# Latents and values of an attention layer in column and row tiles of TensorE

## The reference

```python
q = x @ W_q; k = x @ W_k; v = x @ W_v            # D = 256
latent_kv = (k + v) @ W_down_kv                  # 64 numbers a token
k_rec = (latent_kv @ W_up_k)                     # 16 heads of 16
v_rec = (latent_kv @ W_up_v)
scores = einsum("bhqd,bhkd->bhqk", qh, k_rec) / sqrt(d) * decay
attn = softmax(scores)
out = einsum("bhqk,bhkd->bhqd", attn, v_rec) @ W_o
```

## Time and profile before

| what | value |
|---|---|
| median of the runs | 5883.54 us |
| the profiled execution | 5887.21 us |
| its span, first to last instruction | 5885.3 us |
| mean granted TensorE clock | 0.971 of full speed |
| instructions | 114753 |
| ScalarE busy | 56% of the span |
| VectorE busy | 78% of the span |

### The profile page before, as it was taken

The page is one execution under the profiler, slowest core; times in us unless marked ns, Lnnn a source line. Parts: engine busy times, 40 slices in busy tenths (PEclk is TensorE's granted clock), DMA queues, the critical chain, the costliest instruction groups (busy, mean ns, idle before and its releaser), DMA issues.

```text
span 5885.3 us, 114753 instructions
## 1 busy us (share of the span) xinstructions
PE 5403.7 (92%) x35920; PEld 3230.8 (55%) x35920; DVE 4596.3 (78%) x14385; ACT 3307.3 (56%) x6581; POOL 2830.4 (48%) x2873
## 2 busy tenths in 40 slices
PE   5559999389999999999999999999999999699997
PEld 5558888133444444444444444444444444588886
DVE  7735555577888888888888888888888887555776
ACT  1124444146666666666667666666676666344443
POOL 6740000253647657566475564765756433300455
PEclk9999999688999999999999999999999999799998
DMA  5533333543545555555455454555554543433777
GB/s 173 171 109 105 105 105 102 137 99 77 135 99 129 115 113 123 108 120 126 100 125 115 111 132 103 127 115 111 129 106 111 111 81 67 149 104 119 233 245 228
DMA packets 538508, 731.84 MB, mean 124 GB/s; under 512 B 80281, under 2 KB 454209, under 8 KB 537921
## 3 DMA queue, kind: packets, MB, share of 16 engines
q1 hardware_dynamic: 488768, 590.22, 41.5%
q0 software_dynamic: 49152, 134.28, 7.7%
HBM read 426.70 MB, written 297.53 MB: 123 GB/s over the span
## 4 chain that ended last, share of the span: by engine, by line
PE 70%; POOL 15%; DVE 6%; issue 4%; DMA 3%; SPq 1%; ACT 1%; POOLq 0%; DVEq 0%; ACTq 0%
PE psum L396 13%; PE psum L1315 13%; PE psum L1166 13%; PE psum L1175 10%; PE psum L413 7%; POOL xs L658 4%; PE psum L1179 3%; DVE at_mx L1456 3%; PE psum L385 2%; PE psum L404 2%; POOL at_xT L1616 2%; PE psum L1223 2%; POOL at_Sd L1694 2%; DMA at_xT<-ys,at_yib 2%; POOL at_XR L1625 1%
## 5 line engine op out<-in xcount | busy, mean ns | idle before, releaser
L1379 ACT ACTIVATE at_P<-psum 128x512 f32<-128x512 f32 x4096 | 2125.7, 602 | 981.5 <-PE psum L1175 565.5
L1456 DVE TENSOR_REDUCE at_mx<-psum 128x4 f32<-128x512 f32 x3584 | 2219.1, 681 | 266.1 <-PE psum L1166 260.4
L1166 PE MATMUL psum<-at_kst,at_qst 96*128 96x128 bf16 (+3 forms) x7168 | 1599.0, 293 | 52.3 <-DVE at_mx L1456 29.4
L1175 PE MATMUL psum<-at_qst,at_kst 99*128 99x512 bf16 (+3 forms) x5120 | 1463.5, 319 | 53.8 <-ACT at_P L1379 53.7
L1166 PEld LDWEIGHTS psum<-at_kst,at_qst 96*128 96x128 bf16 x7168 | 617.9, 99 | 1319.4 <-DVE at_mx L1456 509.4
L1315 PE MATMUL psum<-at_P,at_V 128*17 128x512 f32 x8192 | 1092.5, 605 | 0.0
L1694 POOL TENSOR_TENSOR at_Sd<-at_Sd,at_m 128x1024 f32<-128x1024 f32 x256 | 484.2, 1897 | 819.1 <-DVE at_m L1465 818.1
L1175 PEld LDWEIGHTS psum<-at_qst,at_kst 99*128 99x128 bf16 x5120 | 491.4, 98 | 198.8 <-ACT at_P L1379 85.5
L1179 PE MATMUL psum<-at_ident,at_Sd 128*128 128x128 f32 x2048 | 565.8, 276 | 0.0
L1451 DVE CUSTOM_DVE_ANT_0 at_Sd<-psum,at_Dm 128x128 f32<-128x128 f32 x2048 | 443.1, 287 | 90.3 <-PE psum L1166 90.1
L699 POOL DMA_INDIRECT m2Y<-ys,m2yi x256 | 246.8, 964 | 511.5 <-ACT m2X L456 434.0
(11 more groups left out here) (267 smaller groups left out, 8125.5 us busy)
## 6 DMA issues: line engine op xcount, KB each, us to landing
parts<-at_pt SPq DMA_DIRECT2D x768, 128.0 KB
at_qst<-parts SPq DMA_DIRECT2D x768, 128.0 KB
at_kst<-parts SPq DMA_DIRECT2D x128, 384.0 KB
m2X<-xs SPq DMA_DIRECT2D x288, 128.0 KB, 2.4
ys<-m2X SPq DMA_DIRECT2D x288, 128.0 KB, 1.7
m1X<-xs SPq DMA_DIRECT2D x264, 128.0 KB, 2.1
ys<-m1X SPq DMA_DIRECT2D x264, 128.0 KB, 1.7
at_kst<-parts SPq DMA_DIRECT2D x128, 256.0 KB
```

The source lines that it names most:

```text
L1166: ins = e.matmul(bank[z % 4][:, col - 512 * u:col - 512 * u + ln], self.qst[0:96, s, side, 128 * t:128 * t + 128], self.kst[0:96, s, 1 - s ...
L1175: ins = e.matmul(turns[a % 3][:, q0 - 512 * qh:q0 - 512 * qh + ln], self.kst[0:99, s, side, 128 * kb:128 * kb + 128], self.qst[0:99, s, 1 ...
L1379: e.activation(self.P[:, i % NP, 512 * qh:512 * qh + 512], turns[a % 3], ACT.Exp).then_inc(self.taken.sem, 1)
L1456: e.tensor_reduce(self.mx[:, p % 2, hh, 8 * o + 4 * u:8 * o + 4 * u + 4], of, op=ALU.max, axis=AX.X).then_inc(self.s_read.sem, 1)
```

## The change

One latent unit for each batch instead of two. Its eight matmul instructions write the two halves of the partitions of one bank: half ch of the tokens goes to partitions 64 ch to 64 ch + 63 (two column tiles), and lat becomes 128 partitions x 512. The weights W_up_k and W_up_v are loaded twice, into both halves of the partitions. Keys read lat and the weight from the half that belongs to ch, still one bank at a time. Values are issued in pairs: tile t2 of the first half and tile 2 + t2 of the second, as two row tiles that write two turning banks; TensorE waits for one more bank to be read (taken.at(a - 1)), and ScalarE's copies wait until both are filled. The plan has one slot less for latents, and the values stay in four slots, with work in the first and third of them.

```diff
--- before.py
+++ after.py
@@ -719,7 +719,7 @@
         self.qst, self.kst = sb("qst", [99, 2 * NS, 2, S], BF16), sb("kst", [99, 2 * NS, 2, S], BF16)
         self.P, self.Sd = sb("P", [128, NP, S]), sb("Sd", [128, 4, 8, 128])
         self.V = sb("V", [128, 2, 8, H, 17])
-        self.XR, self.xT, self.lat = sb("XR", [128, 8, D]), sb("xT", [128, 2, S]), sb("lat", [DL, S])
+        self.XR, self.xT, self.lat = sb("XR", [128, 8, D]), sb("xT", [128, 2, S]), sb("lat", [128, 512])
         self.qs = sb("qs", [128, 2, 2, 512])
         self.pt = sb("pt", [128, 2, 3, 2, 512], BF16)
         self.OT, self.OF = sb("OT", [128, 2, 8, D]), sb("OF", [128, 2, 512])
@@ -729,7 +729,7 @@
         self.ident, self.Dm = sb("ident", [128, 128]), sb("Dm", [128, 128])
         self.decay = sb("decay", [128, 2, S])
         self.wq, self.wk, self.wo = sb("wq", [128, 2, D]), sb("wk", [128, 2, D]), sb("wo", [128, 2, D])
-        self.wd, self.wuk, self.wuv = sb("wd", [128, 2, DL]), sb("wuk", [DL, D]), sb("wuv", [DL, D])
+        self.wd, self.wuk, self.wuv = sb("wd", [128, 2, DL]), sb("wuk", [128, D]), sb("wuv", [128, D])
         self.wv = self.Ou[:, 0].rearrange("p (k d) -> p k d", k=2)
         self.wT = self.ob[:, 0]
         self.wkv = sb("wkv", [128, 2, DL])
@@ -757,7 +757,7 @@
         self.number()
 
 
-        self.loaded, self.x_in = sig.new("a_loaded", 16 * 15), sig.new("a_x_in", 48 * B)
+        self.loaded, self.x_in = sig.new("a_loaded", 16 * 17), sig.new("a_x_in", 48 * B)
         self.y_in, self.x1_out = sig.new("a_y_in", 256 * B - 128), sig.new("a_x1_out", 16 * B)
         self.y_first = sig.new("a_y_first", 128)
         self.m_out, self.parts_out = sig.new("a_m_out", 16 * NPAIR), sig.ring("a_parts_out", [96 * 4 * B] * 2)
@@ -898,8 +898,7 @@
             yield ("load", b + 1)
 
     def unit_order(self, b):
-        for ch in range(2):
-            yield from (("latent", b, ch), None)
+        yield from (("latent", b), None)
         if not b:
             for i in range(0, 8, 2):
                 yield from (("project", 0, i), ("project", 0, i + 1))
@@ -907,18 +906,18 @@
                     yield from (("cast", 0, i, c), ("cast", 0, i + 1, c), ("rest", 0, i, c), ("rest", 0, i + 1, c))
                 yield from (("send", 0, i), ("send", 0, i + 1))
                 if i == 2:
-                    yield from (("values", 0, t2) for t2 in range(4))
+                    yield from (("values", 0, t2) for t2 in (0, 2, 1, 3))
             return
         for i in range(8):
             yield from (("project", b, i), None, ("cast", b, i, 0), None, ("rest", b, i, 0))
             if i:
                 yield ("send", b, i - 1)
             yield from (None, None, ("cast", b, i, 1), None, ("rest", b, i, 1), None)
-        for t2 in range(4):
-            yield ("values", b, t2)
-            if t2 == 2:
+        for t2 in range(2):
+            yield from (("values", b, t2), ("values", b, 2 + t2))
+            if t2 == 1:
                 yield ("send", b, 7)
-            yield None
+            yield from (None, None)
 
     def norm_order(self, p):
         yield from (None, ("norm", p))
@@ -1069,8 +1068,8 @@
         self.load_tokens(e, 0)
         for dst, src in ((self.ident[:], cst["ident"]), (self.decay[:, 0], cst["decn"]), (self.decay[:, 1], cst["decp"]),
                          (self.Dm[:], cst["dm"]), (self.wq[:], fold(wt["q"])), (self.wk[:], fold(wt["k"])),
-                         (self.wv, fold(wt["v"])), (self.wd[:], fold(wt["down"])), (self.wuk[:], wt["upk"]),
-                         (self.wuv[:], wt["upv"]), (self.wo[:], fold(wt["o"])),
+                         (self.wv, fold(wt["v"])), (self.wd[:], fold(wt["down"])), (self.wuk[0:DL], wt["upk"]), (self.wuk[DL:128], wt["upk"]),
+                         (self.wuv[0:DL], wt["upv"]), (self.wuv[DL:128], wt["upv"]), (self.wo[:], fold(wt["o"])),
                          (self.trif[:], cst["tri"]), (self.misc[:], cst["misc"]), (self.rw[:], fold(wt["rw"])),
                          (self.rb[:], wt["rb"].rearrange("(o n) -> o n", o=1).to_broadcast([128, E]))):
             e.dma_start(dst, src).then_inc(self.loaded.sem, 16)
@@ -1154,7 +1153,7 @@
         NS, NP, V = self.NS, self.NP, bank[4]
         turns = bank[5:8]
         fence(w, self.begin)
-        w.wait_ge(*self.loaded.at(240))
+        w.wait_ge(*self.loaded.at(272))
         w.wait_ge(*self.w_ready.at(2))
 
         def scores(n, o, u, z):
@@ -1204,11 +1203,12 @@
                     ins = e.transpose(to[:, 128 * t:128 * t + 128], self.XR[:, 4 * ch + t, 128 * k:128 * k + 128], self.ident[:])
                 ins.then_inc(self.filled.sem, 1)
             if kind == "latent":
-                b, ch = at
+                b = at[0]
                 w.wait_ge(*self.result("weight", 2))
-                w.wait_ge(*self.result("turn", b, ch, 1))
+                w.wait_ge(*self.result("turn", b, 1, 1))
                 for k in range(2):
-                    ins = e.matmul(to[0:DL, 0:512], self.wkv[:, k, :], self.xT[:, k, 512 * ch:512 * ch + 512], start=(k == 0), stop=(k == 1))
+                    for ch in range(2):
+                        ins = e.matmul(to[DL * ch:DL * ch + DL, :], self.wkv[:, k, :], self.xT[:, k, 512 * ch:512 * ch + 512], start=(k == 0), stop=(k == 1))
                 ins.then_inc(self.filled.sem, 1)
             if kind == "project":
                 b, i = at
@@ -1222,16 +1222,21 @@
                     for k in range(2):
                         ins = e.matmul(of, self.wq[:, k, 128 * hf:128 * hf + 128], self.xT[:, k, sl], start=(k == 0), stop=(k == 1))
                 else:
-                    w.wait_ge(*self.result("latent", b, ch))
-                    ins = e.matmul(of, self.wuk[:, 128 * hf:128 * hf + 128], self.lat[:, sl], start=True, stop=True)
+                    w.wait_ge(*self.result("latent", b))
+                    ins = e.matmul(of, self.wuk[DL * ch:DL * ch + DL, 128 * hf:128 * hf + 128], self.lat[DL * ch:DL * ch + DL, :], start=True, stop=True)
                 ins.then_inc(self.s_filled.sem, 1)
             if kind == "values":
                 b, t2 = at
-                w.wait_ge(*self.result("latent", b, t2 // 2))
-                for j in range(2):
-                    t = 2 * t2 + j
-                    ins = e.matmul(to[:, 256 * j:256 * j + 256], self.lat[:, 128 * t:128 * t + 128], self.wuv[:], start=True, stop=True)
-                ins.then_inc(self.filled.sem, 1)
+                if t2 < 2:
+                    w.wait_ge(*self.result("latent", b))
+                    w.wait_ge(*self.taken.at(a - 1))
+                    for j in range(2):
+                        t = 2 * t2 + j
+                        for half, to in ((0, turns[a % 3]), (1, turns[(a + 1) % 3])):
+                            ins = e.matmul(to[:, 256 * j:256 * j + 256], self.lat[DL * half:DL * half + DL, 128 * t:128 * t + 128],
+                                           self.wuv[DL * half:DL * half + DL, :], start=True, stop=True)
+                            if j == 1:
+                                ins.then_inc(self.filled.sem, 1)
             if kind == "mturn":
                 p = at[0]
                 w.wait_ge(*self.m_max.at(p + 1))
@@ -1337,13 +1342,13 @@
                 w.wait_ge(*self.added.at(2 * b + 2))
                 if b:
                     w.wait_ge(*self.turned_read(b - 1))
-                    w.wait_ge(*self.full("latent", b - 1, 1))
+                    w.wait_ge(*self.full("latent", b - 1))
                 e.activation(self.xT[:, k, 512 * ch:512 * ch + 512], of, ACT.Copy).then_inc(self.taken.sem, 1)
             if kind == "latent":
-                b, ch = at
+                b = at[0]
                 if b:
                     w.wait_ge(*self.full("values", b - 1, 3))
-                e.activation(self.lat[:, 512 * ch:512 * ch + 512], of[0:DL, 0:512], ACT.Copy).then_inc(self.taken.sem, 1)
+                e.activation(self.lat[:], of, ACT.Copy).then_inc(self.taken.sem, 1)
             if kind == "cast":
                 b, i, c = at
                 j = 8 * b + i
@@ -1352,6 +1357,7 @@
                 e.activation(self.pt[:, j % 2, c], self.qs[:, i % 2], ACT.Copy).then_inc(self.part_hi.sem, 1)
             if kind == "values":
                 b, t2 = at
+                w.wait_ge(*self.full("values", b, 2 + t2 % 2))
                 if b >= 2:
                     w.wait_ge(*self.weighed.at(64 * (b - 1)))
                 e.activation(self.V[:, b % 2, 2 * t2:2 * t2 + 2, :, 0:16], of[:, 0:512].rearrange("p (t h d) -> p t h d", t=2, h=H), ACT.Copy).then_inc(self.taken.sem, 1)
```

## The result

The changed kernel takes 5844.2 us (median of 6 runs, 5838.3 to 5855.9), the kernel before, run beside it, 5882.3 us (6 runs, 5878.4 to 5884.4). The ratio is 0.9937, with a 95% interval of 0.9926 to 0.9948: 38 us faster. Forecast were 65, and 5818 us; the measured time lies in the range of 5785 to 5860. The direction held, and so did the latents and most of the pairs; the term for what moves did not.

What follows compares the result with a forecast made beforehand. TensorE was taken to pace most of a batch and GpSimd one stretch; latents 27.9 + 1.8, values 20.4 and what moves 15.4 sum to 65.5 us saved, from 5883.54 to 5818 us, range 5785 to 5860.

Steps and rivals of the forecast that it cites:

- What bounds the kernel: Attention batches: TensorE paces most steps, GpSimd one stretch of some 55 us; TensorE time saved shortens the batch one for one.
- Latents: Merged latent unit on TensorE takes 1.86 us, as one old unit; saves 27.9 us in batches 1 to 15, 1.8 in batch 0.
- (b): Rival: weight loads stand between the column tiles' passes, 16.8 us less saved, 5835 us; chance 0.06.
- (e): Rival: tiles don't run beside each other at all, no saving in latents either, 5876 us; chance 0.04.
- Values: Each pair on TensorE saves 1.05 us less a new wait of 0.37 us: 0.68 us, 20.4 us for 30 pairs.
- rival (a): Row tiles of the values don't overlap; pairs cost +0.32 us instead of -0.68, 5848 us; chance 0.13.
- Rival (c): GpSimd's stretch gets the whole benefit and pairs wait less: -45.5 us instead of -15.4, 5788 us; chance 0.12.
- What moves: One latent slot fewer moves later units a step earlier, changing GpSimd's stretch by -1.1 us a batch, -15.4 us in 14.
- The weakest step named: ScalarE's wait before the cast of project 5 grows, and that is paid back later in GpSimd's stretch.
- Rival (d): The rest of project 6 on GpSimd ends no earlier, as gathers, sends and stack collide: 5903 us; chance 0.07.

Runs made afterwards that it cites:

- g2: The kernel before with both latent units in one slot, so only the plan's shift changes: 5899.4 us, ratio 1.0032, where the kernel before takes 5880.9 us.
- g1: The changed kernel with r_var's addition on GpSimd and the pairs of values behind W: 5825.9 us, ratio 0.9905 to the kernel before.
- h1: The changed kernel with an empty slot behind the latents, r_var's addition on GpSimd and values behind W: 5839.8 us, ratio 0.9919 to the kernel before.
- 6100 groups: Groups of runs in which the kernel before takes some 6100 us (6091.6 and 6111.7 us).
- f3: The changed kernel with r_var's addition moved from VectorE to GpSimd: 5966.3 us, ratio 0.9764 to the kernel before.
- 5880 group: A group of runs in which the kernel before takes some 5880 us.
- the second group: Runs of the changed kernel, in-place part, shift alone and r_var on GpSimd: 5996.0, 6065.2, 6040.4 and 5966.3 us; the kernel before takes 6111.7 us.
- the fourth group: Runs of the changed kernel with empty slot, r_var on GpSimd and values behind W, and with latent loops exchanged: 5839.8 and 5863.7 us; before, 5886.5 us.

## Why the prediction was half right

**What bounds the kernel: right.** TensorE time saved in its regime came off one for one. In the two steps that held latents each batch is 1.9 us shorter.

**Latents: right,** 1.87 us for eight matmuls against 1.86 taken. Rivals (b) and (e) fall with these rows. The Trainium skill's rule on weight loads, which spoke against the change ("TensorE: Matmul & The Clock Gate", Part 3), isn't borne out: with its eight loads between the passes the unit would have been 2.98 us.

**Values: right in kind.** Row tiles overlap as W's column tiles do (1.07 us for eight matmuls), so rival (a) falls. The wait was 0.44 us instead of 0.37: a pair saves 1.05 - 0.02 - 0.44 = 0.59 us, and 30 pairs 17.7, not 20.4. Rival (c) falls too: it wanted shorter waits for the pairs and 3.25 us off a batch for what moves.

**What moves: this step failed.** The forecast was -15.4 us, with bounds of +1.05 and -3.25 a batch; measured alone it is **+18.5 us** (interval +11 to +26), and a batch in steady state is 2.0 us longer, outside the bounds. The step followed the rest of project 6 through GpSimd's queue and the gathered rows through DMA, and both did what it said: that rest ends some 7 us earlier in its batch (5 without the projection that moved across the batch's start), and the add's wait (us, times) fell from

```profile
  DMA at_xT<-ys,at_yib: 35.1, 18
```

in the kernel before to

```profile
  DMA at_xT<-ys,at_yib: 11.8, 2
```

in the changed one. But the sum took the stretch to be as long as that rest decides, and it isn't. TensorE's waits for ScalarE, which hang on the rests, were 31.9 us in 13 batches and fell by 11; its waits for VectorE were 37.4 us and grew by 28. Of VectorE the step said that its small stalls "shift with it: I leave them at zero, bounds +-0.4 us a batch". That sentence was the error, and the trace of before spoke against it: beside the 0.35 us that it read, there was a wait of up to 2.4 us for the maxima in each batch (L1263 above). The add pair moved into a step in which r_stats runs, and there VectorE's r_var waits until GpSimd's add is through, some 2 us, with the maxima and TensorE behind it. The waits come with the shift alone (g2). With r_var on GpSimd the 2.4 us of step 16 are gone (g1), and the shift costs nothing (h1 against g1); both are shown, though both kernels also have the pairs behind W. r_var alone was moved only in 6100 groups, where it gives 30 us (f3). That these waits are all of the shift's cost is not shown: when r_var left, m waited longer in f3, and the stretch of steps 20 to 31 grew in g1 and h1, by 2.1 and 1.5 us.

The Trainium skill has this behaviour ("SBUF — State Buffer", section "Who interferes with whom"): a VectorE instruction with two SBUF inputs, or one such as tensor_scalar in a mode that uses two ports, contends with GpSimd, and the one that is issued later is blocked for the other's whole instruction. The trace agrees for r_var, which ends 0.02 us after the add; in which mode it ran no row shows. A reader of that section would have looked for GpSimd's longest instructions beside each such VectorE instruction. The forecast didn't.

**The weakest step named** was another: that ScalarE's wait before the cast of project 5 would grow. It did not (3.69 us before, 2.05 after):

```profile
2966.00 1.06 ACT L1357 ACTIVATE at_pt<-at_qs 128x1024 bf16<-128x1024 f32 x1 [2.05 <-POOL at_qs L1660]
```

**The balance.** By the starts of W in the two traces, batches 1 to 13 are each 1.49 us shorter: 1.86 for the latent and 1.17 for the pairs off, 1.5 on for what moved (forecast: 1.1 off). That is 13 x 1.49 = 19.4 us. The steps of batch 0 hold two latents, two pairs and one shift, for which the forecast's terms make 6.2; they give 11.9. The shift alone gives 11.2 there (g2), so most of it comes from the plan's start and not from the merged latents. Batch 14 gives 4.5, where 1.4 were forecast for its pairs, and the part ahead of the first W 2.9, where the latents of batch 0 were to give 1.8. The sum, 38.7, is the difference of the two spans (5885.3 - 5846.0 = 39.3) to within 0.6. So 13 x 2.6 = 34 us were missing from the shift's term and 2 from the pairs', and some 10 came back in batch 0, batch 14 and ahead of them. Nothing in the forecast had these 10, so that much of the nearness of 5844 to 5818 is luck.

**Rival (d)** had the sign of the shift's cost right, with the wrong mechanism: it wanted gathered rows that land later, and they land earlier.

**Open.** The in-place part was not run alone in a 5880 group; 38.1 + 18.5 = 56.6 us is what it gives there if the parts add up as they did in the second group. Steps 20 to 31 grow in g1 and h1 by TensorE's waits for ScalarE behind GpSimd's rests; why these rests come later is not known. Nor is it known why the groups differ. The record gives the second and the fourth group the same chip number, 12, though the kernel before takes 6112 us in one and 5887 in the other, so it need not be the chip. Seen is only that in the 6100 groups the parts ahead of the first and behind the last W are longer, and that there the same shift gains 68 to 71 us.

## What to carry to other kernels

A slot that comes free in a written-out plan moves everything behind it: before leaving it out, list for each moved instruction what it will run beside, on other engines too, and try the version that keeps the slot. Where GpSimd makes long instructions on SBUF, a tiny VectorE instruction beside them can cost as much as they last; giving it to GpSimd itself takes that wait away, but look which instruction waits next and what GpSimd then delays: in one version here nothing was gained by it. Tiles of TensorE may be merged by the time of one, and a unit that gains a wait by it belongs behind work that doesn't wait, as the pair behind W.

## What the runs showed of the hardware

- Two column tiles of 64 with fp32 operands take the time of one: eight matmuls of 512 columns in 1.87 us. Their order in the queue doesn't matter (again 1.87 us, and starts in twos 13 ns apart, with four passes of one tile ahead). Two row tiles of 64 rows that write two banks also do: eight matmuls of 256 columns in 1.07 us.
- A tensor_scalar of 128 x 2 on VectorE takes 0.17 us alone and up to 2.24 us beside GpSimd's tensor_tensor of 128 x 1024; a tensor_tensor of 128 x 16 takes 0.17 and up to 2.77 us (in f3_var_pool). In all traces here, the ones of 0.9 us or more end 0.02 to 0.05 us after an instruction of GpSimd's.
- The same kernel took 5881 to 5887 us in three groups of runs and 6092 and 6112 in two, and one edit lost 0.3% in one of the three and gained 1.2% in both of the two. Whether that goes with the chip is not shown.
